# Windowed attention layers: inverse norms of q and k in one chain, the layer norm on two other engines, new step orders

## The reference, cut to what matters

```python
def local_attention(q, k, v):        # windows of 32; each looks at itself and the one before, masked to a band
    ...
def attn_layer(x, Wqkv, qs, ksc, Wo):          # 16 heads of 64
    q, k, v = split(x @ Wqkv, 3)               # by heads
    q = l2norm(q) * qs                         # t / max(norm(t), 1e-12)
    k = l2norm(k) * ksc
    q = q * cos * scale + rotate_half(q) * sin * scale
    k = k * cos / scale + rotate_half(k) * sin / scale
    return heads_joined(local_attention(q, k, v)) @ Wo
def ffn_layer(x, g, bln, W1, b1, W2, b2):
    xn = (x - x.mean(-1)) / sqrt(x.var(-1) + 1e-05) * g + bln
    a, gate = split(xn @ W1 + b1, 2)           # 341 each
    return a * gelu(gate) @ W2 + b2
for i in range(6):
    x = attn_layer(shift_tokens(x), Wqkv[i], q_scale[i], k_scale[i], Wo[i]) + x
    x = ffn_layer(shift_tokens(x), ln_g[i], ln_b[i], W1[i], b1[i], W2[i], b2[i]) + x
```

## Time and profile before

| what | us |
|---|---|
| median of three runs (2050.99 to 2066.19) | 2054.53 |
| the profiled execution | 2048.87 |
| its span in the profile | 2047.1 |

### The profile page before, as it was taken

One profiled execution on the slowest core, in us unless ns is written; L12 is line 12 of the kernel. 1 busy time (PEld: TensorE's weight loads), 2 busy tenths in 40 slices (PEclk: granted clock), 3 DMA queues, 4 the chain that ended last, 5 costly groups with the idle time before them and its releaser, 6 DMA issues. The chain is left out here.

```text
span 2047.1 us, 78950 instructions
## 1 busy us (share of the span) xinstructions
PE 1850.1 (90%) x32837; PEld 1300.6 (64%) x32837; DVE 1440.9 (70%) x2605; ACT 1135.4 (55%) x2379; POOL 1435.4 (70%) x1838
## 2 busy tenths in 40 slices
PE   4769999999999999999999989999999999789858
PEld 3636666666666666666666656666666676556648
DVE  2357778777777777787778867778777787445546
ACT  1135665566566566665566656566656665434425
POOL 1168888778888788788778877888778887412334
PEclk9779999999999999999999999999999999889969
DMA  3021131111311113111113111121111111030012
GB/s 98 0 40 50 47 96 55 42 43 49 101 47 43 49 47 94 50 49 47 46 47 100 51 43 44 34 82 35 27 34 31 37 31 33 10 95 1 22 34 69
DMA packets 60836, 99.93 MB, mean 49 GB/s; under 512 B 15847, under 2 KB 35064, under 8 KB 58642
## 3 DMA queue, kind: packets, MB, share of 16 engines
q1 hardware_dynamic: 58978, 91.72, 15.5%
q0 software_dynamic: 1504, 3.17, 0.5%
HBM read 44.50 MB, written 21.45 MB: 32 GB/s over the span
## 5 line engine op out<-in xcount | busy, mean ns | idle before, releaser
L1273 PE MATMUL b_bank_proj<-layer_weights,b_stream_t 128*128 128x512 f32 x1152 | 616.9, 635 | 21.0 <-DVE b_plain_moved L1069 17.5
L1069 DVE TENSOR_TENSOR b_plain_moved<-b_bank_proj,b_rope 128x1024 f32<-128x1024 f32 x384 | 468.9, 1222 | 210.3 <-ACT b_squares L903 179.2
L812 POOL TENSOR_TENSOR b_rotated<-b_plain_moved 128x1024 f32<-128x1024 f32 x192 | 452.5, 2357 | 42.6 <-DVE b_plain_moved L1069 42.6
L827 POOL TENSOR_TENSOR b_rotated<-b_rotated,b_inv_norm 128x1024 f32<-128x1024 f32 x192 | 365.2, 1902 | 15.4
L903 ACT ACTIVATE b_squares<-b_bank_proj 128x512 f32<-128x512 f32 x384 | 229.6, 598 | 110.2 <-PE b_bank_proj L1273 107.6
L832 POOL TENSOR_TENSOR b_probs<-b_probs,b_inv_sum 128x512 f32<-128x512 f32 x192 | 200.3, 1044 | 81.7 <-DVE b_inv_sum L1090 81.7
L1281 PEld LDWEIGHTS b_bank_shared<-const_tables,b_rotated 128*128 128x128 f32 x1536 | 187.7, 145 | 109.7 <-issue 103.5
L1273 PEld LDWEIGHTS b_bank_proj<-layer_weights,b_stream_t 128*128 128x128 f32 x1152 | 187.8, 195 | 108.7 <-issue 58.5
L1075 DVE TENSOR_REDUCE b_norm<-b_squares 128x16 f32<-128x1024 f32 x192 | 232.2, 1209 | 1.0 <-issue 0.2
L910 ACT ACTIVATE b_v<-b_bank_proj 128x512 f32<-128x512 f32 x192 | 114.5, 596 | 194.3 <-PE b_bank_proj L1273 194.3
L1281 PE MATMUL b_bank_shared<-const_tables,b_rotated 128*128 128x128 f32 x1536 | 210.8, 279 | 2.5 <-POOL b_rotated L827 2.4
(11 more groups left out here) (346 smaller groups left out, 2920.9 us busy)
## 6 DMA issues: line engine op xcount, KB each, us to landing
b_v_shifted<-b_v SPq DMA_DIRECT2D x192, 192.0 KB, 2.4
sorted_rows<-sorted_rows SPq DMA_DIRECT2D x66, 258.0 KB
layer_weights<-L_ffn_Wqkv SPq DMA_DIRECT2D x6, 1536.0 KB
b_v_shifted<-b_v SPq DMA_DIRECT2D x72, 128.0 KB, 3.1
layer_weights<-L_ffn_Wo SPq DMA_DIRECT2D x6, 512.0 KB
c_sorted_in<-sorted_rows SPq DMA_DIRECT2D x23, 129.0 KB, 2.0
layer_weights<-L_ffn_w SPq DMA_DIRECT2D x8, 256.0 KB, 6.1
c_w<-L_ffn_w SPq DMA_DIRECT2D x8, 256.0 KB, 5.9
```

What stands on the lines that cost most here:

```text
L812: nc.gpsimd.tensor_tensor(out=turned[:, k, :], in0=pm[:, k, 0, :], in1=pm[:, k, 1, :], op=ALU.add).then_inc(add_done, 1)
L827: nc.gpsimd.tensor_tensor(out=tk, in0=tk, in1=repeat_last(rn[:, k, :], DH), op=ALU.mult).then_inc(rope_done, 1)
L1069: nc.vector.tensor_tensor(to, src.to_broadcast(shape), tab.to_broadcast(shape), ALU.mult).then_inc(mul_done, 1)
L1273: nc.tensor.matmul(out, xs[:, b, t * P:(t + 1) * P], w, start=True, stop=True).then_inc(proj_full, 1)
```

## The change

For q and k of a slot there is one clamp, one logarithm, one exponential and one Newton chain (`near`) over both in place of two of each; the sums, the inverse norms and the rotated tile get a second buffer, by the slot's parity. The multiplications with the inverse norm stay two (`rope`). `table` of the next layer is made eight slots before the layer begins, ahead of a `rope`, where it was made at its first clamp. The four normalising instructions of the layer norm move from GpSimd to VectorE (`normal`; GpSimd keeps epsilon and power, `inverse`), and the affine part from VectorE to ScalarE (`affine`, in the orders `scale`). All four orders and `FIRST` are new: among other things `heads_t` stand later behind their `project` steps, `out` one slot later, and the steps between `back`, `norm_t` and `up` are others. In the orders below, a list's old lines stand where the text needs them; of the functions, which are printed above as they were, mostly the new lines.

```diff
 PE_TURN = [
...
-    ("project", 2, 3), ("out", -1, 0), ("heads_t", 1, 2), ("heads_t", 1, 3), ("project", 2, 4), ("back", -1, 0),
-    ("probs_t", 0, 0), ("scores", 1, 0), ("project", 2, 5), ("project", 3, 0), ("probs_t", 0, 1), ("project", 3, 1),
-    ("pv", 0, 0), ("project", 3, 2), ("heads_t", 2, 0), ("heads_t", 2, 1), ("project", 3, 3), ("norm_t", -1, 0),
-    ("out", 0, 0), ("up", -1, 0), ("heads_t", 2, 2), ("heads_t", 2, 3), ("up", -1, 1), ("probs_t", 1, 0),
...
+    ("project", 0, 0), ("project", 0, 1), ("out", -4, 0), ("project", 0, 2), ("scores", -2, 0), ("heads_t", -1, 0),
...
+    ("project", 1, 1), ("probs_t", -2, 0), ("down", -2, 0), ("project", 1, 2), ("project", 1, 3), ("scores", -1, 0),
+    ("probs_t", -2, 1), ("heads_t", 0, 0), ("project", 1, 4), ("project", 1, 5), ("heads_t", 0, 1), ("heads_t", 0, 2),
+    ("project", 2, 0), ("project", 2, 1), ("pv", -2, 0), ("heads_t", 0, 3), ("probs_t", -1, 0), ("project", 2, 2),
...
+    ("probs_t", -1, 1), ("enter", 1, 0), ("out", -2, 0), ("project", 3, 0), ("pv", -1, 0), ("heads_t", 1, 0),
+    ("project", 3, 1), ("heads_t", 1, 1), ("out", -1, 0), ("heads_t", 1, 2), ("heads_t", 1, 3), ("back", -1, 0),
+    ("probs_t", 0, 0), ("heads_t", 2, 0), ("project", 3, 2), ("probs_t", 0, 1), ("heads_t", 2, 1), ("project", 3, 3),
+    ("scores", 1, 0), ("norm_t", -1, 0), ("heads_t", 2, 2), ("up", -1, 0), ("up", -1, 1), ("pv", 0, 0), ("up", -1, 2),
+    ("up", -1, 3), ("heads_t", 2, 3), ("project", 3, 4), ("project", 3, 5),
 DVE_TURN = [
...
-    ("residual", 3, 0), ("norms", 6, 1), ("mul", 6, 3), ("stats", 0, 0), ("soft", 5, 0), ("mul", 7, 0), ("mul", 7, 1),
-    ("norms", 7, 0), ("soft", 5, 1), ("mul", 7, 2), ("scale", 0, 0), ("share", 5, 0), ("mul", 7, 3), ("share", 5, 1),
...
+    ("share", 4, 1), ("mul", 7, 0), ("norms", 7, 0), ("residual", 3, 0), ("mul", 7, 1), ("stats", 0, 0),
+    ("mul", 7, 2), ("normal", 0, 0), ("mul", 7, 3), ("soft", 5, 0), ("soft", 5, 1), ("share", 5, 0), ("hidden", 0, 0),
+    ("norms", 7, 1), ("mul", 8, 0), ("norms", 8, 0), ("mul", 8, 1),
 ]
 POOL_TURN = [
...
-    ("clamp", 2, 1), ("weigh", 0, 1), ("add", 2, 1), ("rstd", -1, 0), ("clamp", 3, 0), ("rope", 2, 1),
...
+    ("weigh", -2, 0), ("clamp", 0, 0), ("weigh", -2, 1), ("near", 0, 0), ("rope", 0, 0), ("rope", 0, 1),
+    ("add", 1, 0), ("weigh", -1, 0), ("clamp", 1, 0), ("add", 1, 1), ("add", 2, 0), ("weigh", -1, 1), ("near", 1, 0),
+    ("rope", 1, 0), ("rope", 1, 1), ("clamp", 2, 0), ("weigh", 0, 0), ("near", 2, 0), ("weigh", 0, 1), ("rope", 2, 0),
+    ("add", 2, 1), ("rstd", -1, 0), ("rope", 2, 1), ("add", 3, 0), ("weigh", 1, 0), ("add", 3, 1), ("clamp", 3, 0),
+    ("near", 3, 0), ("rope", 3, 0), ("rope", 3, 1), ("add", 4, 0), ("weigh", 1, 1), ("add", 4, 1),
 ]
...
+    "pe": {("norm_t", TURNS - 1, 0): ("f_weights", "f_contexts",), ("up", TURNS - 1, 5): ("f_normed", "f_keys", "f_queries",),
+            ("down", TURNS - 1, 0): ("f_scores", "leave", "f_counts",)},
+    "act": {
+            ("gelu", TURNS - 1, 2): ("f_weights", "f_contexts", "f_normed", "f_keys", "f_queries", "f_scores", "leave", "f_counts",)},
+    "dve": {("share", SLOTS - 1, 1): ("f_stream",), ("hidden", TURNS - 1, 0): ("f_normed",),
+            ("hidden", TURNS - 1, 2): ("f_own", "f_best",), ("down", TURNS - 1, 0): ("f_counts",)},
+    "pool": {("rope", SLOTS - 12, 0): ("f_fill",), ("rstd", TURNS - 1, 0): ("f_rstd",)},
...
+        ss = m.sb("norm2", [P, 2, 2, HEADS])
...
+        turned = m.sb("rotated", [P, 2, 2, INNER])
...
+                def clamp(u):
+                    pool.wait_ge(ss_done, 2 * u + 2)
+                    wait(pool, prod_done, u - 1)
+                    nc.gpsimd.tensor_scalar(ssc[:, u % 2, :, :], ss[:, u % 2, :, :], 1e-24, None, ALU.max).then_inc(clamp_done, 1)
 
                 def rotate(u, k):
 
                     pool.wait_ge(mul_done, 4 * u + 2 * k + 2)
-                    wait(pool, heads_t_full, 4 * (u - 1) + 2 * k + 2)
...
+                    wait(pool, heads_t_full, 4 * (u - 2) + 2 * k + 2)
+                    nc.gpsimd.tensor_tensor(out=turned[:, u % 2, k, :], in0=pm[:, k, 0, :], in1=pm[:, k, 1, :], op=ALU.add).then_inc(add_done, 1)
+
+                def near(u):
+                    first = rn0[:, u % 2, :, :]
+                    pool.wait_ge(root_done, u + 1)
+                    wait(pool, pow_done, u)
+                    nc.gpsimd.tensor_tensor(out=half_x[:, :, :], in0=first, in1=first, op=ALU.mult).then_inc(half_done, 1)
+                    pool.wait_ge(half_done, u + 1)
+                    nc.gpsimd.tensor_tensor(out=near1[:, :, :], in0=half_x[:, :, :], in1=ssc[:, u % 2, :, :], op=ALU.mult).then_inc(prod_done, 1)
+                    pool.wait_ge(prod_done, u + 1)
+                    nc.gpsimd.tensor_scalar(half_x[:, :, :], near1[:, :, :], -0.5, 1.5, ALU.mult, ALU.add).then_inc(near_done, 1)
+                    pool.wait_ge(near_done, u + 1)
+                    nc.gpsimd.tensor_tensor(out=rn[:, u % 2, :, :], in0=half_x[:, :, :], in1=first, op=ALU.mult).then_inc(pow_done, 1)
 
                 def normed(u, k):
...
+                    pool.wait_ge(pow_done, u + 1)
                     pool.wait_ge(add_done, 2 * u + k + 1)
...
+                    tk = split(turned[:, u % 2, k, :], DH)
+                    nc.gpsimd.tensor_tensor(out=tk, in0=tk, in1=repeat_last(rn[:, u % 2, k, :], DH), op=ALU.mult).then_inc(rope_done, 1)
...
+                def inverse(j):
...
+                table(0)
                 for kind, n, k in steps(POOL_TURN, FIRST["pool"]):
                     if kind == "clamp":
-                        if k == 0 and n % (B * TILES) == 0:
-                            table(n // (B * TILES))
-                        clamp(n, k)
+                        clamp(n)
+                    if kind == "near":
+                        near(n)
                     if kind == "add":
                         rotate(n, k)
                     if kind == "rope":
+                        if k == 0 and n % (B * TILES) == 2 * TILES and n // (B * TILES) + 1 < LAYERS:
+                            table(n // (B * TILES) + 1)
                         normed(n, k)
...
+                def root(u):
+
+                    act.wait_ge(clamp_done, u + 1)
+                    nc.scalar.activation(lnv[:, :, :], ssc[:, u % 2, :, :], ACT.Ln).then_inc(ln_done, 1)
+                    act.wait_ge(ln_done, u + 1)
+                    wait(act, pow_done, u - 1)
+                    nc.scalar.activation(rn0[:, u % 2, :, :], lnv[:, :, :], ACT.Exp, scale=-0.5).then_inc(root_done, 1)
...
+                def affine(j):
+                    l = j // B
+                    if j == 0:
+                        act.wait_ge(const_in, 16 * NC)
+                    act.wait_ge(norm_t_full, j + 1)
+                    wait(act, up_full, 6 * j)
+                    nc.scalar.activation(xnT[:, :], home("norm_t", j)[:, :], ACT.Identity, bias=lnb[:, l:l + 1],
+                                         scale=lng[:, l:l + 1]).then_inc(norm_t_done, 1)
...
+                def normal(j):
+                    dve.wait_ge(rstd_done, j + 1)
+                    for t in range(TILES):
+                        last = nc.vector.tensor_scalar(xn[:, t, :], xn[:, t, :], mv[:, t, 0:1], rstd[:, t:t + 1],
+                                                       ALU.subtract, ALU.mult)
+                    last.then_inc(xn_done, 1)
...
-                        last = nc.tensor.transpose(bank[:, n * P:(n + 1) * P], turned[:, g // 2, at:at + P], ident)
+                        last = nc.tensor.transpose(bank[:, n * P:(n + 1) * P], turned[:, u % 2, g // 2, at:at + P], ident)
```

More of the change, by code:

```diff
@@ L490 @@
 PE_TURN = [
-    ("project", 0, 3), ("scores", -1, 0), ("project", 0, 4), ("probs_t", -2, 0), ("project", 0, 5), ("leave", -3, 0),
-    ("probs_t", -2, 1), ("project", 1, 0), ("heads_t", 0, 0), ("project", 1, 1), ("enter", 1, 0), ("heads_t", 0, 1),
-    ("pv", -2, 0), ("project", 1, 2), ("down", -2, 0), ("heads_t", 0, 2), ("heads_t", 0, 3), ("project", 1, 3),
-    ("project", 1, 4), ("out", -2, 0), ("scores", 0, 0), ("project", 1, 5), ("probs_t", -1, 0), ("project", 2, 0),
-    ("probs_t", -1, 1), ("project", 2, 1), ("heads_t", 1, 0), ("heads_t", 1, 1), ("pv", -1, 0), ("project", 2, 2),
@@ new lines @@
+    ("root", 0, 0), ("project", 1, 1), ("attended", -3, 0), ("attended", -3, 1), ("probs_t", -2, 0),
+    ("project", 1, 2), ("project", 1, 3), ("probs_t", -2, 1), ("project", 1, 4), ("project", 1, 5), ("exp", -1, 0),
+    ("heads_t", 0, 0), ("heads_t", 0, 1), ("project", 2, 0), ("project", 2, 1), ("heads_t", 0, 2), ("exp", -1, 1),
+    ("attended", -2, 0), ("attended", -2, 1), ("probs_t", -1, 0), ("project", 2, 2), ("heads_t", 0, 3),
+    ("project", 2, 3), ("root", 1, 0), ("project", 2, 4), ("exp", 0, 0), ("project", 2, 5), ("leave", -2, 0),
@@ new lines @@
+    ("probs_t", -1, 1), ("exp", 0, 1), ("root", 2, 0), ("project", 3, 0), ("enter", 1, 0), ("attended", -1, 0),
```

(21 more changed lines are left out.)

89 lines of the change are left out of this document (17 added, 72 removed).

## The result

The changed kernel takes 2121.6 us (median; 2111.0 to 2122.9), the one before 2053.7: a ratio of 1.031, with an interval of 1.026 to 1.036. The forecast was 2087 and the range 2036 to 2144. The profiled execution has a span of 2120.6 us, 73.5 more than before. I cut that into turns from `back` to `back` again: the 23 stretches from the first to the last take 1630.9 us and not 1561.3, 3.03 us more in each on average; what lies ahead of the first `back` is 3.6 us longer (218.44 and 214.85), what lies behind the last as long as before (271.2 and 270.9).

What follows compares the result with a forecast made beforehand. PE's own work, about 63.4 us a turn, was taken as the bound. The terms -9 - 4 + 0 + 43 + 6 + 0 = +36 gave 2085 on the profiled execution; forecast 2087 us, range 2036 to 2144.

Steps and rivals of the forecast that it cites:

- What bounds the kernel: PE's own work sets a floor of about 63.4 us a turn; time changes only where PE waits.
- GpSimd's savings, nothing: 7.6 us less GpSimd work a turn, on an engine with 8.7 to spare, gains no time.
- The rope table, -9: Making the table eight slots earlier removes five of six PE waits in `project`: -9 us, bounds 0 and -18.6.
- PE's order at the start, -4: More `project` steps ahead of the first scores cut `project`'s wait outside steady turns: -4 us, bounds 0 and -7.5.
- Instruction reads, 0, with bounds of 15: PE's waits for instruction packets in `pv` and `scores` stay the same: 0 us, bounds +-15.
- The layer norm, +43: `rope(2, 1)` holds up VectorE's `normal`, so PE waits before `norm_t`; with the affine step 2.1 us a turn, net +43.
- the first rival: GpSimd's `add(3, 0)` also gets in and holds up `normal`'s other three instructions: 2144 us, chance 0.15.
- the second block: `add(3, 0)` holding up `normal` after `rope(2, 1)` does: +57 us, 2144 in all, chance 0.15.
- The affine part, 0.6 us a turn: Between `norm_t` and `up`, PE waits for ScalarE's `scale`: 1.45 us, covered by 0.87 of transposes, leaving 0.6.
- The 7 us that were to hide behind reads: Layer norm delay hidden where `scores` stalls for instructions anyway: 0.28 us a turn, -7 us.
- The clock, +6: PE at half clock after pauses: 0.15 us per us of the 43, +6 us, bounds 0 and +29.
- The end, 0: Last turn's norm gains 2.0 us, next stage's preparation gives about as much back: 0, bounds -2 and +4.

Runs made afterwards that it cites:

- the two idle-work runs: The run without a block plus idle GpSimd work directly behind `rstd`: four TENSOR_SCALARs of 128x128, 2025.5 us, or two TENSOR_TENSORs of 128x512, 2076.6 us.
- the run with TENSOR_SCALARs: The run without a block plus four idle GpSimd TENSOR_SCALARs of 128x128 directly behind `rstd`: 2025.5 us, 0.988 of the kernel before.
- the filled pause: The changed kernel with 28 idle transposes on PE directly ahead of `norm_t`'s wait: 2091.5 us, 1.022 of the kernel before.
- The run without a block: The changed kernel with GpSimd's `rope(2, 1)` ahead of `rstd` and `add(3, 0)` waiting for `normal`: 2022.7 us, 0.986 of the kernel before.

## Why the prediction was right, and where it was not

*What bounds the kernel*: right. All that moved the time was PE's waits and PE's clock. *GpSimd's savings, nothing*: right. It is busy for 48.0 us of a quick turn, not 54.65, and the time rose.

*The rope table, -9*: right for the changed kernel. VectorE's waits for it are gone from the steady turns, and PE's 10.0 us there too. Alone it brings some 12 us (0.994 of 2051), but not by the road that I had priced: PE's waits fall only from 10.0 us in `project` to 7.6 in `heads_t`, and the profile, which is of the quickest of its ten executions, has 18.4 us less of busy PE (1831.7). Why PE kept its clock better there is not settled.

*PE's order at the start, -4*: not there. `project`'s wait outside the steady turns is 7.2 us, against 7.5.

*Instruction reads, 0, with bounds of 15*: outside its bounds. The two waits fell by 27.9 us, of which about 22 are reads. The count was right: in the traces 79 packets' boundaries fall in the last two fifths of a `pv` or `scores` before, and 78 after. What I left out is when the read begins, that is, when the packet's transfer starts in the trace. Where it began over 1 us ahead of the step's first matmul, PE lost next to nothing (16 cases before, 34 after, 0.5 us in all); where it began behind it, 0.6 to 2.2 us each (30 cases and 38.9 us before, 22 and 30.2 after). The cases between fell from 33 to 22, and their waits from 19.2 us to 6.2. My reading is that a read starts when PE's sequencer comes into the step, early or late by what the step itself waits for, and that the new order has more steps whose semaphores were set long before; the sequencer's own place isn't in the trace, so this is argued and not shown. The runs agree with it: with `pv` directly behind `scores` the read comes too late in nearly every turn, and with `pv` one `project` later PE waits 10 us less in it.

*The layer norm, +43*: the place, the cause and `rope`'s share were right. In the turn shown, GpSimd's power ends 4.0 us behind `back`, as forecast, and PE is ready for `norm_t` after 5.7 (5.5). The size was not right, because the mechanism was only half of it: `norm_t` waits 3.1 us a turn and not 1.5, since `add(3, 0)` gets in as well. This is the first rival, which had a chance of 0.15 and was to decide if it won in half the turns; it won in 23 of 24. The step that failed is the evidence against it: in the earlier trace rows GpSimd's L1757 did not hold up VectorE's last three, and I took that for any instruction. L1757 is a TENSOR_SCALAR of 128x128, `add` a TENSOR_TENSOR of 128x1024, and the two idle-work runs show that such a difference decides. The meeting with a MEMSET, in which VectorE took 1.62 us, stood in the trace of the kernel before and spoke the other way. The rule of the Trainium skill that I had cited ("SBUF — State Buffer", section "Who interferes with whom") would have given the second block; by the run with TENSOR_SCALARs (1.31 us beside 3.17, with GpSimd first by 0.03) it doesn't hold for every GpSimd instruction. The affine part, 0.6 us a turn, was 0.26 with the block and 0.5 without (6.3 and 12.3 over 24). The 7 us that were to hide behind reads did not: the waits for instructions are 37.9 us with PE held up and 37.8 without.

*The clock, +6*: mis-sized. Busy PE rose by 31.3 us, and the filled pause gives 30 to 45. I had spread the loss of one slow turn over all idle time, and other turns had lost little; a pause of 3 us in every turn brings a stretch of half clock in nearly every turn (0.96 granted over the steady turns, 0.98 before).

*The end, 0*: right, 0.3 us.

So the direction and the place were forecast, and that the time lies inside the range is luck in part. The errors partly cancelled: 32 us too little for the norm (68.3 + 6.3 against 43), 25 too little for the clock, 28 too much for the reads. With the waits in `pv` and `scores` of before the time would be some 2149 (an estimate, 2121.6 + 27.9), beyond the range's 2144.

Not settled: what the joined chain of inverse norms is worth by itself. The run without a block holds the whole change and is 29 us quicker than before. Between the two profiles, PE's waits in `pv` and `scores` fall by 28.0 us, those in `project` by 9.8 and busy PE by 7.5, while the affine part adds 12.3 and `norm_t` 5.5: together 27.5 us less, where the span is 25.8 shorter. Little is left for the chain, but it wasn't run alone.

## What to carry to other kernels

Before an elementwise step moves to VectorE, look at what GpSimd runs in that moment. Here GpSimd's TENSOR_TENSORs of 128x512 and 128x1024 held VectorE's TENSOR_SCALARs up for their whole length, and four TENSOR_SCALARs of 128x128 cost them 0.2 us. One meeting in a trace speaks for the instruction that was met, and not for the next one in the queue. An exchange of two entries of GpSimd's queue and a wait took the meeting away (2121.6 to 2022.7 us, better than before the change). A short pause of the bottleneck in every turn has a second price in its clock, so it is counted more than once. And in this kernel a step of few long matmuls between two of many short ones was worth keeping: back to back, PE stood for its own instructions in 22 of 24 turns.
